# Sliding-window attention layers on one core: the first group of heads of each chunk issued within the chunk before it

## The chip, the cores and the metric

The kernel runs on one core of one Trainium2 chip. The metric is the device time of one execution in microseconds (us); lower is better. PE is the matrix engine (TensorE), DVE the vector engine, ACT the scalar engine, POOL is GpSimd, and SP only issues DMA transfers.

## The reference

Two blocks add up. The first is a gated attention over 4 sequences of 1024 tokens, 16 heads, a window of 64. The second is what the change touches: two transformer layers (`F_DEPTH = 2`), width 256, 8 heads of 64, a window of 128 keys back. Each layer computes

```
h = shift_token(x);  q, k, v = h @ wqkv          # 256 -> 3 x 512
q, k = l2norm(q) * qs, l2norm(k) * ks; rotary positions (xpos) on both
o = softmax(mask(q @ k.T)) @ v                   # per head, local windows
x = x + o @ wo                                   # 512 -> 256
h = layernorm(shift_token(x))
a, g = split(h @ w1 + b1)                        # 256 -> 2 x 682
x = x + (a * gelu(g)) @ w2 + b2                  # 682 -> 256
```

All data is float32. The projections split each operand into a high and a low part and add three products.

## The kernel before

**Two phases.** `attention_phase` does the gated block; the change leaves it alone. `layers_phase` does the two layers for 4 sequences each, so 8 iterations (`it`, `SEQUENCES`), and every iteration has two chunks (`HALVES`) of 512 tokens: 16 chunks in all. A chunk is four tiles of 128 tokens.

**One written order.** The list `ORDER` names the steps of a chunk. Each engine walks through the whole list and does only its own part of each step, in that order; semaphores do the rest. So an engine that waits at one step holds up all its later steps. A step `(kind, a)` counts over both chunks of an iteration.

**The chunk's work.** Attention goes over 8 groups (`UNITS`): 4 pairs of heads times 2 pairs of tiles. For group `a`: `scores` is the product of queries and keys on PE (L1494) and the masked maximum on DVE (L1737); `softmax` is the exponential on ACT (L1649); `weigh` is the reciprocal of the row sums on DVE (L1745) and the scaling on POOL (L1370); `transpose` brings the probabilities across on PE (L1505, L1509) with copies on ACT (L1590, L1593, L1594); `values` multiplies with the values on PE (L1527). `project_o` is the output projection. Then the feed-forward part: `ln_stats`, `ln_apply`, `transpose_h`, 12 steps `up` (L1552) and 12 steps `down` (L1567), and `out` (DVE, L1809), which adds the result to the residual.

**Work for the chunk after.** Within a chunk, the queries, keys and values of the following one are made: `transpose_x` (PE L1422, high part ACT L1602, low part DVE L1688), `project_qk` (PE L1415, ACT L1614 and L1620, DVE L1693), `rope` and `rope_sum`, `transpose_qk` (PE L1466, copied out by ACT L1596 in two copies, queries and keys), `project_v`.

**Buffers that tie the engines.** The scores of even groups lie in one pair of PSUM banks and those of odd groups in another; that second pair is `y_banks` as well, in which `down` adds up. Three more banks (`bank`, handed out in turn by `take_bank`) take the results of all the other PE steps; a fill waits until the fill three before it has been read out. `project_qk`, `transpose`, `transpose_x` and `transpose_qk` take two fills, `project_v` and `up` one.

**The chunk's end.** The order ends with ..., `up 10`, `up 11`, `down 7` to `down 9`, `transpose_qk 3`, `down 10`, `down 11`, `out 0`, `out 1`, and the following chunk starts with `scores 0`, `scores 1`, `transpose_x 0`, `scores 2`, `transpose 0`, `transpose 1`. On DVE `out 1` waits for `down 11`. On PE `scores 0` waits for all four `transpose_qk`, `scores 1` for `out 1`, and `scores 2` for the exponential of group 0.

Of the kernel before, what the change touches and what calls it, by code (L numbers as in the profile page):

```python
# [214 lines left out]
def attention_phase(nc, kept, x, gamma, w_qkv, w_gates, b_gates, w_out, masks, identity, states, attended,  # L215
                    layer_weights, split_weights, tables_in, tables_out, q_scale, k_scale, rows_in, rows_out):

    with ExitStack() as ctx:
# [626 lines left out]
        def _(dve):  # L845
# [127 lines left out]
F_PREPARE = ("load_wqkv", "load_tables", "transpose_x", "project_qk", "rope", "rope_sum", "transpose_qk", "project_v", "cross_values")  # L973
F_FIRST_HALF = ("shift_keys", "load_wqkv", "load_others")
ORDER = [("softmax", 0), ("scores", 0), ("scores", 1), ("weigh", 0), ("weigh", 1), ("softmax", 1), ("load_x1", 0), ("transpose_x", 0),
         ("scores", 2), ("transpose", 0), ("softmax", 2), ("transpose", 1), ("load_x", 0), ("scores", 3), ("weigh", 2), ("project_qk", 0),
         ("weigh", 3), ("softmax", 3), ("rope", 0), ("scores", 4), ("values", 0), ("values", 1), ("take_o", 0), ("transpose", 2),
         ("project_qk", 1), ("scores", 5), ("weigh", 4), ("rope_sum", 0), ("softmax", 4), ("transpose", 3), ("project_qk", 2),
         ("values", 2), ("scores", 6), ("weigh", 5), ("load_tables", 0), ("load_others", 0), ("shift_keys", 0), ("rope", 1), ("softmax", 5),
         ("values", 3), ("transpose_qk", 0), ("take_o", 1), ("transpose", 4), ("softmax", 6), ("scores", 7), ("shift_front", 0),  # L980
         ("weigh", 6), ("project_qk", 3), ("project_o", 0), ("transpose", 5), ("softmax", 7), ("rope_sum", 1), ("weigh", 7), ("values", 4),
         ("values", 5), ("take_o", 2), ("transpose", 6), ("project_v", 0), ("transpose_qk", 1), ("transpose", 7), ("ln_stats", 0),
         ("ln_apply", 0), ("take_o", 3), ("rope", 2), ("values", 6), ("values", 7), ("project_v", 2), ("transpose_h", 0), ("project_o", 1),
         ("rope_sum", 2), ("up", 0), ("up", 1), ("ln_stats", 1), ("up", 2), ("project_v", 1), ("down", 0), ("down", 1), ("project_v", 3),
# [6 lines left out]
def layers_phase(nc, kept, attended_end, states, attended, out, wqkv_in, wo_in, w1_in, w2_in, rows_in, tables_in, masks):  # L991
# [3 lines left out]
    with ExitStack() as ctx:  # L995
# [333 lines left out]
        def _(pool):  # L1329
# [565 lines left out]
```

## Time and profile before

| | |
|---|---|
| median of 3 runs | 1958.6 us (1950.5 to 1962.69) |
| the profiled execution: own time | 1963.61 us |
| its span, first to last instruction | 1961.8 us |
| granted TensorE clock, mean | 0.981 of full speed |
| the layers' part of the span | about 707 to 1961 us |
| PE busy | 94% of the span |
| ACT, DVE, POOL busy | 70%, 64%, 47% |

The profile is one execution. Busy shares are over the whole span; they do not tell which engine holds up a given stretch, so the views that follow are cut to the end of one chunk. A row of the timeline reads: start in us, duration, engine, line of the kernel, operation, what it writes and reads, how many, and in brackets how long the engine was idle before it and what ended that. A PE row that joins many matmuls ends about 0.2 us after the next one could start, since matmuls overlap.

### The profile page before, as it was taken

How to read it: one execution, taken by the hardware profiler on the slowest of the kernel's cores; microseconds unless marked ns; L12 is line 12 of the kernel's file. 1: busy time of each engine (PE TensorE's matmuls, PEld its weight loads, DVE VectorE, ACT ScalarE, POOL GpSimd, SP SyncE). 2: the span in 40 equal slices, each digit the busy share in tenths (PEclk: the TensorE clock that was granted, in tenths of full speed). 3: DMA queues.
4: the chain of work that ended last, by engine and by line, in shares of the span. 5: the costliest groups of instructions: out<-in, count | busy, mean ns of one | idle time of the engine just before them, and what ended most of it. 6: DMA issues, size and time to landing. Idle time of an engine off the chain costs nothing.

```text
span 1961.8 us, 47822 instructions
## 1 busy us (share of the span) xinstructions
PE 1842.9 (94%) x17808; PEld 1567.0 (80%) x17808; DVE 1246.3 (64%) x4125; ACT 1376.9 (70%) x3997; POOL 922.5 (47%) x1315
## 2 busy tenths in 40 slices
PE   6999999999999689999999999999999999999998
PEld 4788788788788469788788897887888878878777
DVE  4544543454443367777777777677777777777765
ACT  5886987878688365866757758667576585775764
POOL 2533543444344454636536446355364563654632
PEclk9999999999999889999999999999999999999999
DMA  4321320322324610110110101304112112010110
GB/s 146 99 76 56 116 87 34 116 76 77 88 78 146 196 41 23 47 55 23 47 43 24 55 15 53 122 15 166 39 39 63 34 47 65 25 54 25 44 45 28
DMA packets 127003, 128.91 MB, mean 66 GB/s; under 512 B 28112, under 2 KB 101940, under 8 KB 126772
## 3 DMA queue, kind: packets, MB, share of 16 engines
q1 hardware_dynamic: 123604, 119.56, 19.7%
q10 hardware_dynamic: 3168, 6.29, 0.9%
q8 instruction: 142, 2.33, 0.5%
q14 instruction: 89, 0.73, 0.1%
HBM read 72.84 MB, written 37.25 MB: 56 GB/s over the span
## 4 chain that ended last, share of the span: by engine, by line
PE 41%; DVE 11%; ACT 11%; issue 1%; POOL 1%; DMA 1%; SPq 0%; DVEq 0%; ACTq 0%; POOLq 0%
PE f_bank L1415 17%; PE f_bank L1552 7%; PE f_o_bank L1527 4%; PE f_scores L1567 4%; PE f_scores L1494 3%; ACT f_prob L1649 3%; DVE f_u L1803 3%; DVE f_gu L1799 2%; PE f_bank L1505 2%; ACT f_u L1669 2%; PE f_bank L1466 2%; PE f_bank L1509 1%; ACT f_probT L1590 1%; DVE f_actT L1688 1%; ACT f_probT L1594 1%
## 5 line engine op out<-in xcount | busy, mean ns | idle before, releaser
L594 POOL TENSOR_SCALAR a_prob<-a_prob,a_row_inv,a_gate 128x128 f32<-128x128 f32 x512 | 227.6, 468 | 377.7 <-DVE a_row_inv L932 377.7
L1370 POOL TENSOR_SCALAR f_prob<-f_prob,f_row_inv 128x192 f32<-128x192 f32 x512 | 214.5, 443 | 291.6 <-DVE f_row_inv L1745 291.6
L1415 PE MATMUL f_bank<-weights,f_actT 128*128 128x512 f32 x1152 | 302.9, 409 | 5.4 <-DVE f_norm L1693 3.9
L1552 PE MATMUL f_bank<-f_hT,f_w 128*128 128x256 f32 x2112 | 270.2, 283 | 5.4 <-DVE f_gu L1799 5.4
L1552 PEld LDWEIGHTS f_bank<-f_hT,f_w 128*128 128x128 f32 x2112 | 259.4, 189 | 10.3 <-DVE f_gu L1799 8.9
L1415 PEld LDWEIGHTS f_bank<-weights,f_actT 128*128 128x128 f32 x1152 | 211.7, 193 | 55.4 <-DVE f_norm L1693 7.7
L1352 POOL TENSOR_TENSOR f_qk_tok<-f_qk_tok,tables 128x512 f32<-128x512 f32 x128 | 165.1, 1313 | 158.4 <-DVE f_sin_part L1705 158.4
L1649 ACT ACTIVATE f_prob<-f_scores,f_neg_max 128x192 f32<-128x192 f32 x512 | 208.5, 428 | 14.1 <-DVE f_neg_max L1737 12.8
L1346 POOL TENSOR_TENSOR f_norm<-f_norm,f_minus_half 128x16 f32<-128x16 f32 x64 | 199.3, 3115 | 34.0 <-DVE f_norm L1697 32.4
L1669 ACT ACTIVATE f_u<-f_gu 128x256 fp32r<-128x256 f32 x192 | 80.3, 418 | 191.2 <-DVE f_gu L1799 191.2
L824 ACT ACTIVATE a_prob<-a_scores,a_neg_max 128x128 f32<-128x128 f32 x512 | 179.9, 392 | 24.0 <-DVE a_neg_max L923 17.0
L615 PE MATMUL a_bank<-a_xT,weights 128*128 128x512 f32 x768 | 195.0, 404 | 1.5 <-DVE a_wgate L901 1.5
L1737 DVE CUSTOM_DVE_ANT_0 f_scores<-f_scores,f_mask 128x192 f32<-128x192 f32 x512 | 166.2, 387 | 36.4 <-PE f_scores L1494 36.1
L1803 DVE TENSOR_TENSOR f_u<-f_gu,f_u 128x256 fp32r<-128x256 f32 x192 | 114.5, 596 | 93.0 <-ACT f_u L1669 93.0
L615 PEld LDWEIGHTS a_bank<-a_xT,weights 128*128 128x128 f32 x768 | 142.5, 190 | 36.7 <-issue 2.9
L1567 PE MATMUL f_scores<-f_w,f_u 128*128 128x256 f32 (+1 forms) x1088 | 153.3, 285 | 0.6 <-DVE f_u L1803 0.3
L923 DVE CUSTOM_DVE_ANT_0 a_scores<-a_scores,a_mask 128x128 f32<-128x128 f32 x512 | 129.9, 325 | 25.8 <-PE a_scores L689 25.8
L1567 PEld LDWEIGHTS f_scores<-f_w,f_u 128*128 128x128 f32 (+1 forms) x1088 | 139.5, 189 | 5.3 <-DVE f_u L1803 3.8
L1494 PEld LDWEIGHTS f_scores<-f_kT,f_q 64*64 64x64 f32 x3072 | 101.1, 140 | 43.6 <-ACT f_prob L1649 19.8
L1494 PE MATMUL f_scores<-f_kT,f_q 64*64 64x128 f32 (+2 forms) x3072 | 120.0, 290 | 16.2 <-ACT f_prob L1649 15.5
L1665 ACT ACTIVATE f_gu<-f_bank,f_rows 128x256 f32<-128x256 f32 x192 | 89.8, 468 | 53.3 <-PE f_bank L1552 52.0
L1693 DVE TENSOR_REDUCE f_norm<-f_square 128x8 f32<-128x512 f32 x128 | 86.0, 683 | 61.4 <-ACT f_square L1620 61.3
(139 smaller groups left out, 3988.8 us busy)
## 6 DMA issues: line engine op xcount, KB each, us to landing
split_weights<-a_hi_lo SPq DMA_DIRECT2D x16, 512.0 KB
x_next<-states SPq DMA_DIRECT2D x32, 256.0 KB, 4.4
tables<-scaled_tables SPq DMA_DIRECT2D x16, 512.0 KB, 5.4
f_x<-states SPq DMA_DIRECT2D x16, 512.0 KB, 3.8
split_weights<-a_hi_lo SPq DMA_DIRECT2D x12, 682.0 KB
weights<-split_weights ACTq DMA_DIRECT2D x6, 1024.0 KB, 9.9
f_w<-split_weights SPq DMA_DIRECT2D x4, 1280.0 KB, 10.6
f_v_crossed<-f_v SPq DMA_DIRECT2D x40, 128.0 KB, 2.3
```

What stands on the lines that cost most here:

```text
L594: last = nc.gpsimd.tensor_scalar(part, part, row_inv[:, a % 2, head, t:t + 1], gate[:, half, t, h:h + 1], ALU.mult, ALU.mult)
L615: last = nc.tensor.matmul(out, lhs(c, a), rhs(c, b), start=(i == 0), stop=(i == len(order) - 1))
L824: e = nc.scalar.activation(prob[:, a % 2, head, t, :], scores[a % 2][head][:, t, :], ACT.Exp, bias=neg_max[:, a % 2, head, t:t + 1], scale ...
L1346: nc.gpsimd.tensor_tensor(n, n, minus_half[:], ALU.pow).then_inc(norm_ready.sem, 1)
L1370: last = nc.gpsimd.tensor_scalar(part, part, row_inv[:, a % 2, head, t:t + 1], 1.0, ALU.mult, ALU.mult)
L1415: last = nc.tensor.matmul(out, lhs(c, a), rhs(c, b), start=(i == 0), stop=(i == len(order) - 1))
L1494: mm = nc.tensor.matmul(scores[a % 2][head][queries, t, place:place + keys.stop - keys.start], q[rows, pair, col:col + P][:, queries], kT[ ...
L1552: mm = nc.tensor.matmul(out[:, which * PART:(which + 1) * PART], w1[:, wp, c, col:col + P], hT[:, hp, c, columns_of(a // FH)], start=(i == ...
L1567: mm = nc.tensor.matmul(y_banks[a // FH % PARTS][:, t, :], u[0:k, a % GATED, up, t * P:(t + 1) * P], w2[0:k, wp, j, :], start=(j == 0 and ...
L1649: last = nc.scalar.activation(prob[:, a % 2, head, t, :], scores[a % 2][head][:, t, 0:KEYS], ACT.Exp, bias=neg_max[:, a % 2, head, t:t + 1 ...
L1737: last = nc.vector.tensor_tensor_reduce(out=sc, in0=sc, in1=mask[:, t + 1 if half or tile or t else 0], scale=-1.0, scalar=3e38, op0=ALU.a ...
L1803: nc.vector.tensor_tensor(place, gu[0:m, a % 2, :], u[0:m, a % GATED, HI, :].bitcast(F32), ALU.subtract).then_inc(u_ready.sem, 1)
```

## The change

**What is moved.** Group 0 of the following chunk becomes step 8 of the chunk: `scores 8`, `softmax 8` and `weigh 8` stand at the end of `ORDER`, and `scores 0`, `softmax 0`, `weigh 0` are gone from its start. `transpose_qk 3`, which stood between `down 9` and `down 10`, now stands after `down 11`. The other steps of the list are placed anew as well; per engine the order is, apart from group 0 and `transpose_qk 3`:

```
PE:   values 2 goes from behind project_qk 2 to ahead of transpose 3; the rest as before
ACT:  ... up 11, softmax 8, transpose_qk 3 | softmax 1, transpose_x 0, transpose 0 ...
      (before: ... up 11, transpose_qk 3 | softmax 0, softmax 1, transpose_x 0, transpose 0 ...)
DVE:  ... up 11, out 0, out 1, scores 8, weigh 8 | scores 1, weigh 1, transpose_x 0 ...
      (before: ... up 11, out 0, out 1 | scores 0, scores 1, weigh 0, weigh 1, transpose_x 0 ...)
POOL: weigh 8 comes last in the chunk, weigh 1 first in the following one
SP:   load_x1, load_tables, load_others, shift_front, shift_back, load_x, cross_values, shift_keys,
      add_attended, out  (before: load_x second, shift_keys ahead of shift_front)
```

**The waits.** The first group waits only for the first two tiles of queries and keys, group 4 for all four. Waits for weights and rows that are loaded once in a layer are made once in a layer.

```diff
+F_ATTENTION = ("scores", "softmax", "weigh")
...
-         ("transpose_qk", 3), ("down", 10), ("down", 11), ("out", 0), ("out", 1), ("load_wqkv", 0)]
+ORDER = [("scores", 1), ("weigh", 1), ("softmax", 1), ("transpose_x", 0), ("scores", 2), ("transpose", 0), ("softmax", 2), ("transpose", 1),
...
+         ("up", 6), ("up", 7), ("down", 4), ("up", 8), ("up", 9), ("rope_sum", 3), ("down", 5), ("down", 6), ("x1_bias", 0),
+         ("add_attended", 0), ("transpose_qk", 2), ("up", 10), ("up", 11), ("out", 0), ("out", 1), ("scores", 8), ("load_wqkv", 0),
+         ("softmax", 8), ("down", 7), ("down", 8), ("down", 9), ("down", 10), ("down", 11), ("weigh", 8), ("transpose_qk", 3)]
...
-                  ("transpose_qk", t0 + 3)]
+                  ("transpose_qk", t0 + 3), ("scores", NU), ("softmax", NU), ("weigh", NU)]
...
             half, s = divmod(a, UNITS)
-            return half, s % PAIRS, s // PAIRS * 2
+            return half % HALVES, s % PAIRS, s // PAIRS * 2
...
+        def before_unit(it, a):
+
+            sequence, unit = started(it, a - 2)
+            return sequence, ("scores", unit)
+
+        def started(it, a):
+
+            return (it, a) if a else (it - 1 if it else None, NU)
...
+        LAYER_STARTS = (0, BATCH)
...
                 elif kind == "project_qk":
                     if a % TILES == 0:
-                        pe.wait_ge(kept.weights_loaded[QUERY], loads(1, layer))
-                        pe.sem_inc(pe_carried, 1)
+                        if fresh:
+                            pe.wait_ge(kept.weights_loaded[QUERY], loads(1, layer))
+                            pe.sem_inc(pe_carried, 1)
                         pe.wait_ge(emptied.sem, emptied.past(it, ("transpose_x", a // TILES), CT - 1))
                     for which in (QUERY, KEY):
-                        if which == KEY and a % TILES == 0:
+                        if which == KEY and a % TILES == 0 and fresh:
                             pe.wait_ge(kept.weights_loaded[KEY], loads(1, layer))
                             pe.sem_inc(pe_carried, 1)
...
                 elif kind == "project_v":
-                    pe.wait_ge(kept.weights_loaded[2], loads(1, layer))
+                    if fresh:
+                        pe.wait_ge(kept.weights_loaded[2], loads(1, layer))
...
+            def take_scores(it, a):
+
+                half, pair, tile = unit_place(a)
+                chunk, s = divmod(a, UNITS)
+                if s == 0:
+
+                    pe.wait_ge(copied.sem, copied.past(it, ("transpose_qk", (chunk - 1) * TILES + 1), 1))
+                    if half:
+                        pe.wait_ge(keys_shifted.sem, keys_shifted.past(it, ("shift_keys", 0)))
+                elif s == 1:
+                    pe.wait_ge(x2_ready.sem, x2_ready.upto(it, 2 * half - 1))
+                elif s == PAIRS:
+
+                    prepared_in = it if half else it - 1 if it else None
+                    pe.wait_ge(copied.sem, copied.past(prepared_in, ("transpose_qk", (half or HALVES) * TILES - 1), 1))
+
+                if s == 1 and a < UNITS:
+                    pe.wait_ge(exped.sem, exped.past(it - 1, ("scores", NU - 1), 1) if it else exped.upto(None, -1))
+                elif it is not None:
+                    pe.wait_ge(exped.sem, exped.past(*before_unit(it, a), 1))
+                for t in (0, 1):
...
+                mm.then_inc(scored.sem, 1)
```

`weigh` (POOL), `softmax` (ACT), `masked_max` and `invert` (DVE) are the bodies of before, moved into functions so that the list `before` can call them too. `before`, the steps ahead of the first iteration, gets the first group of the first chunk; the last iteration leaves out its `scores 16`.

## Rows read from the trace of the kernel before

**Rows 1.** The page, part 1: busy time, share of the span and instructions of each engine.

```profile
...
PE 1842.9 (94%) x17808; PEld 1567.0 (80%) x17808; DVE 1246.3 (64%) x4125; ACT 1376.9 (70%) x3997; POOL 922.5 (47%) x1315
...
```

**Rows 2.** What PE waited for between 780 and 1962 us: total us, times, longest.

```profile
...
PE f_scores L1494 <- ACT f_prob L1649: 15.5, 17, 2.0
PE f_bank L1505 <- POOL f_prob L1370: 12.6, 32, 1.2
...
PE f_bank L1509 <- DVE f_actT L1688: 4.2, 14, 0.3
PE f_bank L1415 <- DVE f_norm L1693: 3.7, 14, 0.3
...
```

**Rows 3.** All engines in order of time at one chunk's end, 1416.3 to 1424.5 us.

```profile
...
1416.41 0.60 ACT L1596 ACTIVATE f_q<-f_bank 128x512 f32<-128x512 f32 x1
...
1416.87 1.49 DVE L1809 TENSOR_TENSOR f_x<-f_scores,f_x 128x512 f32<-128x512 f32 x2
...
1416.90 0.59 ACT L1596 ACTIVATE f_kT<-f_bank 128x512 f32<-128x512 f32 x1
1417.51 1.28 ACT L1649 ACT_TABLE_LOAD   x1
...
1417.56 1.75 PE L1494 MATMUL f_scores<-f_kT,f_q 64*64 64x192 f32 x48
...
1418.71 0.37 DVE L1737 CUSTOM_DVE_ANT_0 f_scores<-f_scores,f_mask 128x192 f32<-128x192 f32 x1 [0.36 <-PE f_scores L1494]
...
1419.23 1.09 PE L1422 MATMUL f_bank<-ident,x_next 128*128 128x128 f32 x8
...
1419.48 0.42 ACT L1649 ACTIVATE f_prob<-f_scores,f_neg_max 128x192 f32<-128x192 f32 x1 [0.69 <-DVE f_neg_max L1737]
...
1421.24 0.18 DVE L1745 RECIPROCAL f_row_inv<-f_row_sum 128x4 f32<-128x4 f32 x1
...
1421.26 0.89 PE L1494 MATMUL f_scores<-f_kT,f_q 64*64 64x192 f32 x24 [0.93 <-ACT f_prob L1649]
...
1421.62 3.24 POOL L1370 TENSOR_SCALAR f_prob<-f_prob,f_row_inv 128x192 f32<-128x192 f32 x8 [12.92 <-DVE f_row_inv L1745]
...
1422.27 0.45 ACT L1649 ACTIVATE f_prob<-f_scores,f_neg_max 128x192 f32<-128x192 f32 x1
...
1422.59 0.41 PE L1505 MATMUL f_bank<-ident,f_prob 128*128 128x128 f32 x2 [0.45 <-POOL f_prob L1370]
1422.67 1.12 ACT L1602 ACTIVATE f_actT<-f_bank 128x512 fp32r<-128x512 f32 x2
...
1422.85 0.18 DVE L1745 RECIPROCAL f_row_inv<-f_row_sum 128x4 f32<-128x4 f32 x1 [1.44 <-ACT f_prob L1649]
...
1423.34 1.29 DVE L1688 TENSOR_TENSOR f_actT<-f_bank,f_actT 128x512 fp32r<-128x512 f32 x2 [0.31 <-ACT f_actT L1602]
...
1424.09 0.44 PE L1509 MATMUL f_bank<-ident,f_prob 128*128 128x128 f32 x2 [0.34 <-DVE f_actT L1688]
...
```

**Rows 4.** PE at the third tile's query product of the same chunk.

```profile
...
1437.63 3.06 PE L1415 MATMUL f_bank<-weights,f_actT 128*128 128x512 f32 x12 [0.27 <-DVE f_norm L1693]
...
```

**Rows 5.** Four chunks, `out` to `out`: length, busy us (instructions), clock, DMA, GB/s.

```profile
...
1495.87:1574.13 78.26, 74.49 (x736) 64.65 (x736) 59.13 (x165) 54.07 (x151) 42.18 (x48) 1.00 0.16 48
1653.16:1732.89 79.73, 76.01 (x737) 65.71 (x736) 59.41 (x164) 54.07 (x151) 42.19 (x48) 0.98 0.16 48
1574.13:1653.16 79.03, 75.19 (x769) 65.56 (x768) 60.13 (x164) 54.39 (x151) 42.89 (x48) 1.00 0.14 43
1732.89:1813.13 80.24, 76.55 (x768) 66.69 (x768) 60.08 (x165) 54.42 (x151) 42.86 (x48) 0.98 0.14 42
...
```

**Rows 6.** Four us behind two chunk ends: length, PE busy, clock, DMA, GB/s.

```profile
...
1739.89:1743.89 4.00, 3.78 (x33) 0.57 0.99 304
1820.13:1824.13 4.00, 3.63 (x39) 1.00 0.64 241
...
```

**Rows 7.** The page, part 6: one DMA issue, KB each, us to landing.

```profile
...
x_next<-states SPq DMA_DIRECT2D x32, 256.0 KB, 4.4
...
```

More of the change, by code:

```diff
@@ L973 @@
 F_PREPARE = ("load_wqkv", "load_tables", "transpose_x", "project_qk", "rope", "rope_sum", "transpose_qk", "project_v", "cross_values")
+F_ATTENTION = ("scores", "softmax", "weigh")
 F_FIRST_HALF = ("shift_keys", "load_wqkv", "load_others")
[L975 to L984, printed above, removed]
-         ("ln_apply", 1), ("up", 3), ("down", 2), ("transpose_h", 1), ("rope", 3), ("up", 4), ("down", 3), ("up", 5), ("up", 6), ("up", 7),
-         ("down", 4), ("up", 8), ("up", 9), ("x1_bias", 0), ("rope_sum", 3), ("down", 5), ("down", 6), ("transpose_qk", 2),
-         ("shift_back", 0), ("up", 10), ("up", 11), ("down", 7), ("down", 8), ("cross_values", 0), ("down", 9), ("add_attended", 0),
-         ("transpose_qk", 3), ("down", 10), ("down", 11), ("out", 0), ("out", 1), ("load_wqkv", 0)]
@@ L1054, in layers_phase @@
                     steps.append((kind, h * PER_CHUNK[kind] + i))
-        last = [(kind, a) for kind, a in steps if kind != "load_x" and not (kind in F_PREPARE and (a >= (HALVES - 1) * PER_CHUNK[kind] or kind == "load_wqkv"))]
+        last = [(kind, a) for kind, a in steps if kind != "load_x" and not (kind in F_ATTENTION and a == NU) and not (kind in F_PREPARE and (a >= (HALVES - 1) * PER_CHUNK[kind] or kind == "load_wqkv"))]
         e, t0 = HALVES - 1, (HALVES - 1) * TILES
@@ L1360, in _ @@
                     rope(None, a)
+                elif kind == "weigh":
+                    weigh(None, a)
             def iteration(it, steps, layer):
@@ L1475, in iteration @@
                 for kind, a in steps:
[L1476 removed]
+                    ahead = a // PER_CHUNK[kind] == HALVES - 1
+                    if kind not in F_ATTENTION:
+                        prepare(it, kind, a, next_layer if ahead else layer, ahead and it == BATCH - 1)
                     if kind == "scores":
[L1478 to L1497 removed]
+                        take_scores(it, a)
                     elif kind == "transpose":
@@ L1628, in _ @@
                     take_raw(None, a)
+                elif kind == "softmax":
+                    softmax(None, a)
             def iteration(it, steps, layer, next_layer):
@@ L1726, in _ @@
                     rope_sum(None, a)
-            dve.wait_ge(consts_loaded, 16 * CONSTS)
+                elif kind == "scores":
+                    dve.wait_ge(consts_loaded, 16 * CONSTS)
+                    masked_max(None, a)
+                elif kind == "weigh":
+                    invert(None, a)
             def iteration(it, steps, layer):
```

123 lines of the change are left out of this document (68 added, 55 removed).

## The prediction

> **What bounds the kernel now.** I began with the page: PE is busy 94% of the span, no other engine over 70% [rows 1]. So what a change in the order can win is PE's idle time, and what it can lose is more of it. The second view is what PE waited for in the layers [rows 2]. The reader should see that the waits are few and all alike: 15.5 us in 17 waits of `scores` for ACT's exponential, 12.6 us in 32 waits of `transpose` for POOL, 4.2 us in 14 waits of L1509 for the low part of `transpose_x` on DVE, and 3.7 us in 14 waits of a query product for DVE's sums of squares. 14, 32 and 17 against 15 chunk ends say where they lie: the first three repeat at every chunk end, the fourth once in a chunk.
>
> The third view is one such end in order of time [rows 3]. PE runs through `scores 0` and `scores 1` (from 1417.56), then `transpose_x` (from 1419.23), is idle 0.93 us until `scores 2` at 1421.26, idle 0.45 before the first transpose at 1422.59, and waits again for L1509 at 1424.09. What ends that last wait is a chain on other engines: masked maximum on DVE at 1418.71, eight exponentials on ACT from 1419.48 to 1422.67 (groups 0 and 1, 0.40 each), `transpose_x` high part on ACT at 1422.67, its low part on DVE at 1423.34, then L1509. PE's own work in that stretch is cover, not the limit. Idle per end: 0.93 + 2 x 12.6/32 + 4.2/14 = 2.0 us.
>
> **The change part by part.**
>
> *The masked maximum of group 0.* It now follows `out 1` directly. DVE ends `out 0` and `out 1` at 1416.87 + 1.49 = 1418.36 and then waits 0.36 us for `scores` on PE [rows 3]. With the scores done before `down 7`, that wait goes and nothing more: `out 1` stands ahead of `scores 8` in DVE's order and waits for `down 11`. So on DVE, and behind it on ACT and POOL, group 0 does not lie inside the preceding chunk. Gain 0.35 us per end. What is late next is `out 1` itself.
>
> *PE around it.* `scores 8` takes the place of `transpose_qk 3` between `up 11` and `down 11`. Two groups of scores take 1419.23 - 1417.56 = 1.67 us, 0.84 each; eight transposes show as 1.09 with 0.2 of tail, so about 0.87 [rows 3]. The swap moves `down 11` by 0.03 us at most; I cost it at nothing. The downs that lose this cover still have `scores 8` in its place.
>
> *The copies of `transpose_qk 3`.* Here I see the cost. On ACT they stand at 1416.41 and 1416.90, while ACT has nothing else to do: the exponential waits 0.69 us for DVE even after them [rows 3]. After the change they stand behind `softmax 8`, which waits for the masked maximum, and ahead of `softmax 1`. They enter the chain. Queued behind them on ACT are `softmax 1`, `transpose_x` and the copies of `transpose 0`; and PE's second fill of `transpose_x` waits for the first copy, since it gets that bank.
>
> By the rows: the maximum starts at 1418.36, the exponential 0.77 later as now (1419.48 - 1418.71) at 1419.13, its four parts end at 1420.73, and the copies, 0.49 each (from 1416.41 to 1416.90), at 1421.71.
>
> *The reciprocal ahead of the second maximum.* DVE now does `weigh 8` before `scores 1`. The fourth part of the exponential starts at 1420.33; the reciprocal follows such a start by 0.58 (1422.27 to 1422.85), so 1420.91; it takes 0.18; the maximum of group 1 follows, and its exponential 0.77 later: 1421.86. That is a shade later than the copies allow. The exponential of group 1 therefore starts at 1421.86, against 1419.48 + 4 x 0.40 = 1421.08 now: 0.78 later. Everything behind it moves as one: high part, low part, L1509. POOL starts `weigh 8` earlier, but `weigh 1`, which the second transpose needs, starts with that same 0.78.
>
> Bounds: if the reciprocal overlaps the next maximum by half, 0.69; if both copies cost the 0.61 that the second shows before the table load, 1421.95 and so 0.87. I take 0.78, by the rows of the same instructions. Over 15 ends: 11.7 us. At the last of them `transpose_x` is absent, but POOL's `weigh 1` sets the same shift. For the start of the first chunk, which no row here shows, I allow -1 to +1 and take 0.
>
> *The table load.* ACT loads the exponential's table in 1.28 us at 1417.51, and the exponential starts 1.97 us after that start, held by DVE [rows 3]. After the change the load stands directly behind `up 11`, at 1416.41, and costs nothing. The Trainium skill, "ScalarE: Activation LUTs", section "What ACT_TABLE_LOAD costs", counts a drain on top, 2.66 us for a switch. By that the load would be what binds now (1417.51 + 2.66 = 1420.17), moving it up would win 1.04 instead of 0.35 per end, and the sum would be about 10 us better. The row has an exponential at 1419.48, so it disagrees, and I go by the row.
>
> *`values 2` ahead of `transpose 3`.* PE waits 0.27 us at 1437.63 for a bank that DVE empties [rows 4]; the moved step takes longer than that and fills the gap. Gain: all of the 3.7 us [rows 2]. Bound: 0 if its own operand were late.
>
> *Waits made once in a layer.* They are for data that landed long before; no row of [rows 2] names such a wait. Cost and gain 0; bound of gain 2 us.
>
> *SP's order.* `load_x` and its two transfers, 4.4 us to landing [rows 7], go behind `shift_back`, and `cross_values` and `shift_keys` behind them. `transpose_x` needs the rows only in the following chunk; the DMA engines are busy 0.14 to 0.16 of a chunk [rows 5], and that is the cover. If it were gone, `ln_stats 1` would wait up to those 4.4 us. I take 0.
>
> *The clock.* The granted clock behind a chunk end is 0.57 to 0.73 at eleven of the ends and 1.00 at four, all in the second layer; one of each kind is in [rows 6]. The levels are 1.2 and 2.4 GHz. What it costs: chunks alike but for that take 79.73 against 78.26 and 80.24 against 79.03, so 1.2 to 1.5 us [rows 5]. In front of every fall stand the idle pieces above. The change lengthens them, from 2.0 to 2.8 us per end, with one piece of about 1.6 before the second half of `transpose_x`. Bounds: none of the four further ends falls (0), all do (5.4), or low stretches get twice as long (15 x 1.35 = 20 more). I take two of four: 2.7.
>
> **Sum.** 11.7 - 3.7 + 2.7 = +10.7 us. Against the profiled execution's own 1963.6 (its span of 1961.8 with 1.8 around it) that is 1974.3. The median of the runs is 5.0 below that execution, so 1958.6 + 10.7 = 1969.
>
> **The rivals.**
>
> *A, the forecast:* copies in the chain, clock a little worse. 1962 to 1977. Chance 0.53.
>
> *B, the clock decides.* The longer idle pieces let the clock fall behind all ends, and for longer at most of them: 8.0 + 5.4 + 10 to 20, so 1982 to 1992; in its mildest form 1979. For it: eleven of fifteen fall already. Against it: four ends with the very same idle pieces did not fall. Chance 0.25.
>
> *C, faster: the copies stay off the path.* If the bank and ACT's queue are no limit after all, because `scores 2` and POOL's first scaling, both 0.35 us earlier, are what set the pace, the end becomes 15 x 0.35 = 5.3 shorter; with the 3.7 that is -9.0, 1950. It decides where the delay at L1509 is under 3.7/15 = 0.25 us. For it: PE waits for ACT and POOL are three quarters of the idle time [rows 2]. Against it: L1509 waits too, last in the chain. Chance 0.17.
>
> *D, the change does what it is called.* Attention of the following chunk really runs beside the feed-forward part and all idle pieces at the ends go: 15 x 2.0 + 3.7 = 34 us, 1925. It needs the masked maximum ahead of `out 1`, which DVE's order excludes. Chance 0.05. The Trainium skill, "Perfetto Trace Analysis", section "Optimization Strategy", says that interleaving regimes with different limits may improve performance; that speaks for D, and the order of [rows 3] does not let it happen here.
>
> **The numbers.** About 1% is what a measurement of this kernel tells from no change: 1939 to 1978. D is faster (0.05), A and C are within (0.70), B is slower (0.25). The range takes in A, C and the lower part of B: 1949 to 1984. A alone is 1962 to 1977.
>
> **What would show it.** In the timeline of a chunk end after the change: the masked maximum directly behind `out 1`, without a wait; the two copies of L1596 between the fourth and fifth exponential; a PE gap of about 1.6 us within `transpose_x` and `scores 2` about 0.5 us later after `out 0` than now (4.39 us); L1509 8.0 us after the start of `out 0` instead of 7.22. The wait of 0.27 at the third query product gone. Chunks 0.5 us longer at equal clock; 1.00 behind fewer than four ends. I am wrong if the copies are found before the exponential, if L1509 comes earlier than 7.22, or if a chunk's length changes by something that does not sit at its end.

## The result

The changed kernel takes 1962.9 us, the median of 19 executions (1960.8 to 1965.8); the kernel before took 1957.8 on the same chip (19 executions, 1950.5 to 1962.7). The ratio is 1.0033, with a 95% interval of 1.0025 to 1.0041: 5 us slower, within 1%. The prediction was 1969 with a range of 1949 to 1984. Case A stood at 1962 to 1977, so the time is at its lower edge. That it lies there is partly luck: the order of the work cost more than forecast, the granted clock gave time back where it was forecast to cost some, and the two errors nearly cancel.

Waits of PE in the layers of the changed kernel (us in total, times, longest), to be held against [rows 2]:

```profile
PE f_bank L1445 <- ACT f_q L1637: 19.4, 14, 1.4
PE f_bank L1550 <- DVE f_actT L1735: 18.8, 14, 1.3
PE f_bank L1546 <- POOL f_prob L1379: 10.9, 19, 1.3
...
PE f_scores L1519 <- ACT f_prob L1668: 1.5, 1, 1.5
...
```

The exponential's 15.5 us are gone but for the 1.5 at the last end, and so are the 3.7 for the sums of squares. In their place stand two waits of a new kind, for the copies of `transpose_qk 3` (1.4 each end) and for the low part of `transpose_x` (1.3).

One chunk end in order of time (start, duration, engine, line), where [rows 3] showed the end before. `out` is now L1868, the masked maximum L1773, the exponential L1668, the copies L1637, the reciprocal L1781, and the transpose that closed the chain, L1509, is L1550:

```profile
1411.13 1.28 ACT L1668 ACT_TABLE_LOAD   x1
1411.14 0.42 DVE L1862 TENSOR_TENSOR f_u<-f_gu,f_u 42x256 fp32r<-42x256 f32 x1 [0.48 <-ACT f_u L1716]
1411.59 1.49 DVE L1868 TENSOR_TENSOR f_x<-f_scores,f_x 128x512 f32<-128x512 f32 x2
...
1413.00 0.35 DVE L1773 CUSTOM_DVE_ANT_0 f_scores<-f_scores,f_mask 128x192 f32<-128x192 f32 x1
...
1415.36 0.61 ACT L1637 ACTIVATE f_q<-f_bank 128x512 f32<-128x512 f32 x1
1415.51 0.18 DVE L1781 RECIPROCAL f_row_inv<-f_row_sum 128x4 f32<-128x4 f32 x1 [1.15 <-ACT f_prob L1668]
1415.67 0.37 DVE L1773 CUSTOM_DVE_ANT_0 f_scores<-f_scores,f_mask 128x192 f32<-128x192 f32 x1
1415.83 0.62 ACT L1637 ACTIVATE f_kT<-f_bank 128x512 f32<-128x512 f32 x1
...
1416.02 0.66 PE L1445 MATMUL f_bank<-ident,x_next 128*128 128x128 f32 x4 [1.38 <-ACT f_q L1637]
...
1416.44 0.42 ACT L1668 ACTIVATE f_prob<-f_scores,f_neg_max 128x192 f32<-128x192 f32 x1
...
1419.43 0.44 PE L1550 MATMUL f_bank<-ident,f_prob 128*128 128x128 f32 x2 [1.34 <-DVE f_actT L1735]
```

The order is the predicted one: maximum directly behind `out 1`, copies between the fourth exponential and the fifth (1416.44), a PE gap of 1.38 (forecast: about 1.6) inside `transpose_x`. The idle pieces of PE at an end sum to 2.7 us instead of 2.0. L1550 starts 7.84 us behind `out 0`; before it was 7.22.

Two chunks of the second layer, `out` to `out` (length, busy us and instructions of PE, PEld, DVE, ACT, POOL, then clock, DMA share, GB/s), against [rows 5]:

```profile
1411.59:1492.23 80.64, 75.25 (x770) 65.59 (x768) 60.41 (x164) 54.20 (x151) 43.92 (x48) 1.00 0.14 42
1492.23:1570.76 78.53, 74.15 (x738) 64.65 (x736) 59.28 (x165) 53.88 (x151) 42.04 (x48) 1.00 0.16 48
```

The two chunks of an iteration differ in length: one has about 770 PE instructions, the other about 738. At a clock of 1.00 the short kind is 0.27 us longer than before (78.53 against 78.26), near the 0.35 that the chunk end gives: +0.62, less the 0.27 of the query product. The long kind is 1.6 longer (80.64 against 79.03). That is not at its end, but 41 us behind it:

```profile
1446.25 2.64 POOL L1379 TENSOR_SCALAR f_prob<-f_prob,f_row_inv 128x192 f32<-128x192 f32 x4
...
1447.39 1.22 DVE L1759 TENSOR_TENSOR f_qk_tok<-f_qk_tok,f_sin_part 128x1024 f32<-128x1024 f32 x1
...
1448.71 1.25 DVE L1762 TENSOR_TENSOR f_qk_tok<-f_qk_tok,f_norm 128x1024 f32<-128x1024 f32 x1
1448.87 3.87 POOL L1362 TENSOR_TENSOR f_norm<-f_norm,f_minus_half 128x16 f32<-128x16 f32 x1
...
1452.73 1.79 POOL L1379 TENSOR_SCALAR f_prob<-f_prob,f_row_inv 128x192 f32<-128x192 f32 x4
1453.69 0.41 PE L1546 MATMUL f_bank<-ident,f_prob 128*128 128x128 f32 x2 [0.71 <-POOL f_prob L1379]
...
1454.58 0.44 PE L1546 MATMUL f_bank<-ident,f_prob 128*128 128x128 f32 x2 [0.47 <-POOL f_prob L1379]
```

PE waits 0.71 + 0.47 us in the seventh transpose for POOL's `weigh 7`, because `weigh 6` took 2.64. The same place before the change shows 1.66 and no wait:

```profile
1450.90 1.66 POOL L1370 TENSOR_SCALAR f_prob<-f_prob,f_row_inv 128x192 f32<-128x192 f32 x4
...
1452.48 1.22 DVE L1712 TENSOR_TENSOR f_qk_tok<-f_qk_tok,f_sin_part 128x1024 f32<-128x1024 f32 x1
1452.49 3.98 POOL L1346 TENSOR_TENSOR f_norm<-f_norm,f_minus_half 128x16 f32<-128x16 f32 x1
```

Last, the clock behind two chunk ends of the changed kernel, the second being the one end where it falls ([rows 6] are those of before):

```profile
1417.59:1421.59 4.00, 2.50 (x36) 1.81 (x35) 2.74 (x11) 3.68 (x14) 1.62 (x4) 1.00 0.57 211
1894.83:1898.83 4.00, 2.67 (x16) 1.70 (x20) 1.53 (x9) 3.96 (x17) 1.62 (x4) 0.56 0.22 76
```

The granted clock stays at 1.00, the upper level of 2.4 GHz, behind 14 of the 15 ends; before the change it fell behind eleven. So at equal clock seven chunks cost 1.5 more and seven 0.3 more, 12.6 us; the last, shorter one 1.6 more (68.08 against 66.45, its clock lower in both). The two spans differ by -0.9, which leaves about 15 us to have come back; 10 falls fewer at the 1.2 to 1.5 each of [rows 5] would be 12 to 15. The profiled execution before was slower than any of the 19 (1963.6 against at most 1962.7), which is why the medians show +5 where the two profiled executions show -0.9. More falls than usual would explain it, but the clocks of those 19 are not on record.

### The profile page after: what moved, and what is told of

The parts are those of the page before. It is cut to its first block, busy times and chain, and to the rows that moved or that the text cites. A ratio compares the mean times of both kernels' runs of the same rounds, so it can differ in the third digit from the quotient of the medians.

```text
span 1960.9 us, 47748 instructions
## 1 busy us (share of the span) xinstructions
PE 1828.5 (93%) x17808; PEld 1558.8 (79%) x17808; DVE 1250.1 (64%) x4125; ACT 1372.4 (70%) x3997; POOL 928.6 (47%) x1315
## 4 chain that ended last, share of the span: by engine, by line
PE 35%; DVE 12%; ACT 11%; POOL 5%; issue 4%; DVEq 0%; SPq 0%; POOLq 0%; ACTq 0%
PE f_bank L1438 14%; PE f_bank L1593 7%; PE f_scores L1608 4%; ACT f_prob L1668 4%; PE f_o_bank L1568 3%; DVE f_u L1862 3%; PE f_scores L1519 3%; DVE f_gu L1858 2%; POOL f_prob L1379 2%; PE f_bank L1546 2%; ACT f_u L1716 2%; POOL f_norm L1362 1%; POOL f_qk_tok L1368 1%; DVE f_actT L1735 1%; DVE f_scores L1773 1%
## 5 line engine op out<-in xcount | busy, mean ns | idle before, releaser
L1379 POOL TENSOR_SCALAR f_prob<-f_prob,f_row_inv 128x192 f32<-128x192 f32 x512 | 220.0, 449 | 288.6 <-DVE f_row_inv L1781 288.6
L1593 PEld LDWEIGHTS f_bank<-f_hT,f_w 128*128 128x128 f32 x2112 | 259.6, 189 | 10.9 <-DVE f_gu L1858 9.5
L1668 ACT ACTIVATE f_prob<-f_scores,f_neg_max 128x192 f32<-128x192 f32 x512 | 208.3, 424 | 25.0 <-DVE f_neg_max L1773 23.8
L1773 DVE CUSTOM_DVE_ANT_0 f_scores<-f_scores,f_mask 128x192 f32<-128x192 f32 x512 | 166.9, 387 | 20.8 <-PE f_scores L1519 20.7
L1608 PE MATMUL f_scores<-f_w,f_u 128*128 128x256 f32 (+1 forms) x1088 | 149.0, 285 | 0.3 <-DVE f_u L1862 0.3
L936 DVE TENSOR_TENSOR a_o<-a_o_bank,a_o 128x512 fp32r<-128x512 f32 x64 | 44.1, 689 | 118.7 <-ACT a_o L831 118.7
```

Source lines behind the costliest of these rows:

```text
L1379: last = nc.gpsimd.tensor_scalar(part, part, row_inv[:, a % 2, head, t:t + 1], 1.0, ALU.mult, ALU.mult)
L1593: mm = nc.tensor.matmul(out[:, which * PART:(which + 1) * PART], w1[:, wp, c, col:col + P], hT[:, hp, c, columns_of(a // FH)], start=(i == ...
L1608: mm = nc.tensor.matmul(y_banks[a // FH % PARTS][:, t, :], u[0:k, a % GATED, up, t * P:(t + 1) * P], w2[0:k, wp, j, :], start=(j == 0 and ...
L1668: last = nc.scalar.activation(prob[:, a % 2, head, t, :], scores[a % 2][head][:, t, 0:KEYS], ACT.Exp, bias=neg_max[:, a % 2, head, t:t + 1 ...
L1773: last = nc.vector.tensor_tensor_reduce(out=sc, in0=sc, in1=mask[:, t + 1 if half or tile or t else 0], scale=-1.0, scalar=3e38, op0=ALU.a ...
```

## The experiments

Twelve kernels ran, in groups of four on a chip each; the kernel before took 1958.8, 1957.9 and 1961.6 in the three groups. So the ratios compare best; a difference of two medians from different groups can hold some 4 us of the chip. "Norms late" means that POOL does the norms of `project_qk 3` behind `weigh 7` (e2). The chunk lengths are those of the second layer.

| run | median us | ratio to before, 95% | mean clock | long, short chunk at 1.00 |
|---|---|---|---|---|
| before | 1957.8 to 1961.6 | 1 | 0.982 | 79.03, 78.26 |
| after | 1962.9 | 1.0033 (1.0025 to 1.0041) | 0.989 | 80.5, 78.5 |
| e1 `values 2` alone | 1961.2 | 1.0012 (1.0000 to 1.0025) | 0.984 | 79.92, 78.02 |
| e11 the same, norms late | 1956.3 | 0.9993 (0.9978 to 1.0007) | 0.982 | 78.58, 78.01 |
| e2 after, norms late | 1954.4 | 0.9976 (0.9963 to 0.9989) | 0.989 | 79.17, 78.48 |
| e3 copies back | 1999.3 | 1.0199 (1.0183 to 1.0215) | 0.973 | none |
| e5 reciprocal back | 1958.5 | 1.0005 (0.9992 to 1.0018) | 0.990 | 80.44, 78.51 |
| e4 both back | 1959.6 | 1.0003 (0.9989 to 1.0018) | 0.987 | 80.12, 78.21 |
| e6 maximum before `out` | 1968.3 | 1.0051 (1.0030 to 1.0072) | 0.984 | 80.05, 78.13 |
| e8 early maximum, norms late | 1962.0 | 1.0021 (1.0007 to 1.0035) | 0.985 | 79.33, 78.61 |
| e16 before, transposes twice | 1956.5 | 0.9974 (0.9963 to 0.9986) | 0.986 | 79.02, 78.37 |
| e14 e11, transposes twice | 1950.8 | 0.9941 (0.9927 to 0.9954) | 0.987 | 78.64, 78.00 |
| e13 e5, norms late | 1951.8 | 0.9945 (0.9932 to 0.9957) | 0.989 | 79.13, 78.45 |
| e10 e4, norms late | 1949.5 | 0.9933 (0.9920 to 0.9946) | 0.988 | 78.86, 78.18 |

The mean clock is over all executions of a run; within the kernel before, 0.001 of it goes with 1.05 to 1.75 us, by the group; 1.35, used below, is a middle value and what rests on it an estimate.

### Where the long chunks come from

**e1_values2_alone.** The kernel before, with this in its order:

```diff
-("softmax", 4), ("transpose", 3), ("project_qk", 2), ("values", 2), ("scores", 6)
+("softmax", 4), ("values", 2), ("transpose", 3), ("project_qk", 2), ("scores", 6)
```

> The kernel before with one part of the change: in the order, `values 2` stands ahead of `transpose 3` and `rope_sum 0`. My step (0.27 us per chunk): the wait of 0.27 us of the query product for DVE's sums of squares goes, 3.7 us over the layers, and each chunk is 0.27 shorter at equal clock. Rival (the move costs elsewhere): the step gives POOL or DVE another place in the chunk, and the seventh transpose then waits for POOL's `weigh 7` in every other chunk, as in the changed kernel; then at least 7 of the chunks are about 1 us longer than now and the sum is +3 to +4.

The rival was right, by the chunks; the time itself hardly shows it (the interval of the ratio begins at 1.0000). The wait of 0.27 is gone and the short chunks are 0.24 shorter, but the long ones are 0.9 longer. POOL is not late here:

```profile
1446.84 2.66 POOL L1370 TENSOR_SCALAR f_prob<-f_prob,f_row_inv 128x192 f32<-128x192 f32 x4
...
1447.99 1.22 DVE L1712 TENSOR_TENSOR f_qk_tok<-f_qk_tok,f_sin_part 128x1024 f32<-128x1024 f32 x1
...
1449.47 3.87 POOL L1346 TENSOR_TENSOR f_norm<-f_norm,f_minus_half 128x16 f32<-128x16 f32 x1
```

`weigh 6` starts 34.03 us behind `out 0` (1412.81), exactly as before (1450.90 - 1416.87). DVE's addition comes 0.43 earlier: 1.15 us behind `weigh 6` instead of 1.58. `weigh 6` is four scalings of about 0.41, so the fourth starts 1.2 us in. With 1.58 it is under way before the addition; with 1.15 the addition is first, the fourth scaling stands until it ends (1447.99 + 1.22 = 1449.21) and finishes at 1449.5. In the changed kernel the distance is 1.14, so there too it is the `values 2` move that makes the long chunks, not the chunk end. The short chunks are spared because their distance there is 1.38, and the fourth scaling starts first:

```profile
1525.96 1.63 POOL L1379 TENSOR_SCALAR f_prob<-f_prob,f_row_inv 128x192 f32<-128x192 f32 x4
...
1527.34 1.32 DVE L1759 TENSOR_TENSOR f_qk_tok<-f_qk_tok,f_sin_part 128x1024 f32<-128x1024 f32 x1
```

The Trainium skill, "SBUF — State Buffer", section "SBUF: two separate sides", has the rule: a DVE instruction with two SBUF inputs and a GpSimd instruction that reads SBUF take a shared port as a lock, and whichever comes second stands for the whole of the first. For POOL behind DVE the rows agree, with 1.0 us per meeting. For DVE behind POOL they show less than the whole: the addition above takes 1.32 instead of 1.22, and the DVE instruction that starts inside the norms before the change (L1715 at 1453.81, the norms from 1452.49 to 1456.47) takes its usual 1.23. Before the change the norms met the addition and paid it (3.98); now `weigh 6` pays it once and the norms once more, on L1762 (3.87).

**e2_norms3_behind_weigh7.** The changed kernel; POOL skips the norms of tile 3 at their place and does them behind `weigh 7`:

```diff
 if kind == "weigh":
     weigh(it, a)
+    if a % UNITS == UNITS - 1 and ("project_qk", late) in steps:
+        norms(it, late)
 elif kind == "project_qk":
-    norms(it, a)
+    if a % TILES != TILES - 1:
+        norms(it, a)
```

> The changed kernel with one thing moved: POOL computes the norms of `project_qk 3` (3.87 us) behind its `weigh 7` instead of ahead of it. Theory (POOL's chain of `weigh 4` to `weigh 7` ends 0.62 us later behind the chunk end, and in every other chunk its `weigh 6` then runs beside DVE's addition of `rope_sum 1` and takes 2.64 instead of 1.66 us): the waits of 0.71 and 0.47 us of transpose 7 for `weigh 7` go, seven chunks become 1.1 us shorter, sum -7 to -8 against the changed kernel, 1955. Rival 1 (the time only shifts): the norms are now late for `rope 3` or for `transpose_qk`, and the wait shows there; 0. Rival 2 (the extra 1.1 us is not POOL's): the waits go and the chunks stay as long as they are; 0.

Faster by 8.6 us in the medians and by 11 in the ratios (0.9976 against 1.0033), against 7 to 8 in the theory; seven chunks of 1.33 are 9.3:

```profile
1442.62 2.63 POOL L1379 TENSOR_SCALAR f_prob<-f_prob,f_row_inv 128x192 f32<-128x192 f32 x4
...
1447.23 1.63 POOL L1379 TENSOR_SCALAR f_prob<-f_prob,f_row_inv 128x192 f32<-128x192 f32 x4 [1.98 <-DVE f_row_inv L1785]
1448.82 2.92 POOL L1362 TENSOR_TENSOR f_norm<-f_norm,f_minus_half 128x16 f32<-128x16 f32 x1
```

`weigh 6` still takes 2.63, but POOL is now idle for 1.98 before `weigh 7`, which comes in time. The norms meet no addition and take 2.92, the price without a collision. The expectation's reason, POOL late by 0.62, is wrong: in e1 POOL is not late and the chunks are long all the same. The cure did not depend on it.

**e11_values2_norms3.** The edits of e1 and e2 together, on the kernel before.

> The kernel before with `values 2` ahead of `transpose 3` and POOL's norms of `project_qk 3` behind its `weigh 7`. Alone, the first made seven chunks 0.9 us longer (79.9 against 79.0 at equal clock), with POOL's `weigh 6` at 2.66 instead of 1.66 us beside DVE's addition of `rope_sum 1`, and the others 0.22 shorter. Theory (that overlap and what it delays is the whole of it): `weigh 6` still takes 2.6, but `weigh 7` no longer stands behind the norms; no wait for it is left, both kinds of chunk are 0.22 to 0.27 shorter than in the kernel before, so about -5.5 against the run with `values 2` alone, 1955 to 1956. Rival (the longer chunks come from PE's own order, the scaling is only seen beside it): seven chunks stay near 79.9, 1961.

Both kinds of chunk are now shorter than before, by 0.45 and 0.25 (78.01), and POOL is busy for 42.73 us of the long one instead of the 43.78 of e1 (before: 42.86):

```profile
1409.33:1487.91 78.58, 75.09 (x768) 65.57 (x768) 60.10 (x165) 54.19 (x151) 42.73 (x48) 1.00 0.14 43
```

The median gains 4.9 on e1 (theory: 5.5), the ratio 0.19%, or 3.7 us. Seven chunks of 1.34 are 9.4, and the clock, 0.982 against 0.984, takes a part of it. Why the long kind gains 0.18 beyond the 0.27 is not traced.

### What sets the chunk end

**e3_transpose_qk3_back** and **e4_both_back**, from the changed kernel:

```diff
-("softmax", 8), ("down", 7), ("down", 8), ("down", 9), ("down", 10), ("down", 11), ("weigh", 8), ("transpose_qk", 3)]
+("down", 7), ("down", 8), ("down", 9), ("transpose_qk", 3), ("softmax", 8), ("down", 10), ("down", 11), ("weigh", 8)]
```

and in e4 also `weigh 8` gone from there, with `("weigh", 0)` behind `("scores", 1)`.

> The changed kernel with `transpose_qk 3` back between `down 9` and `down 10`, and ACT's exponential of group 0 behind its copies, so that the copies stand ahead of the chain and not in it; the reciprocal stays ahead of the second maximum. Theory of the prediction (both paths, copies and reciprocal, end at nearly the same time, so that taking away one gives little): PE's idle piece of 1.38 us inside `transpose_x` goes, L1550 comes no more than 0.1 us earlier behind the start of `out 0` than the 7.84 of the changed kernel; sum 0 to -2. Rival (the copies alone are the delay): L1550 comes 0.4 to 0.6 earlier, 15 x 0.5 = -7.5.

> The changed kernel with both taken out of the chain: `transpose_qk 3` as before the change, and the reciprocal and POOL's scaling of group 0 behind the maximum of group 1. Theory (0.62 us of delay per end is copies and reciprocal together, and the masked maximum directly behind `out 1` is a gain of its own of 0.35 to 0.43): L1550 at 6.8 us behind the start of `out 0` against 7.84 now and 7.22 before the change; POOL is no longer late, so that the waits of transpose 7 for `weigh 7` go too; 15 x 1.05 + 7 x 1.1 = -23 against the changed kernel at equal clock, 1940; if the granted clock falls again behind eleven of the ends as before the change, 11 x 1.35 = +15, so 1955. Rival (something else sets the end, as `scores 2` or POOL's first scaling): L1550 at 7.2 or later, -9 at equal clock, 1954 to 1969.

Neither kernel takes only the copies off the chain: with `scores 8` still ahead of `down 7`, the transposes now delay `down 11`. One end of e3:

```profile
1434.12 0.69 DVE L1868 TENSOR_TENSOR f_x<-f_scores,f_x 128x512 f32<-128x512 f32 x1
...
1435.66 0.69 DVE L1868 TENSOR_TENSOR f_x<-f_scores,f_x 128x512 f32<-128x512 f32 x1 [0.84 <-PE f_scores L1608]
...
1436.27 0.36 DVE L1773 CUSTOM_DVE_ANT_0 f_scores<-f_scores,f_mask 128x192 f32<-128x192 f32 x1
...
1439.72 0.42 ACT L1668 ACTIVATE f_prob<-f_scores,f_neg_max 128x192 f32<-128x192 f32 x1 [0.97 <-DVE f_neg_max L1773]
...
1442.70 0.69 PE L1550 MATMUL f_bank<-ident,f_prob 128*128 128x128 f32 x2 [1.42 <-DVE f_actT L1735]
```

`out 1` waits 0.84 (0.11 in the changed kernel), and PE 0.78 for the bank that it empties, so everything behind `out 1` is 0.73 late. Counted from `out 0`, L1550 comes at 8.58, less that 0.73 at 7.85, against 7.84: the copies alone are worth nothing. In e4, with the reciprocal out as well, the end is this (`out 0` at 1408.56; L1772 is the maximum, L1667 the fifth exponential, L1549 the transpose):

```profile
1410.71 0.35 DVE L1772 CUSTOM_DVE_ANT_0 f_scores<-f_scores,f_mask 128x192 f32<-128x192 f32 x1
...
1413.07 0.43 ACT L1667 ACTIVATE f_prob<-f_scores,f_neg_max 128x192 f32<-128x192 f32 x1
...
1416.06 0.44 PE L1549 MATMUL f_bank<-ident,f_prob 128*128 128x128 f32 x2 [0.34 <-DVE f_actT L1734]
```

The transpose comes at 7.50, less 0.73 at 6.77: together the two are worth 1.07 (theory 1.05). Counted from the masked maximum, nothing has to be taken off: the fifth exponential follows it by 2.38 before the change, 3.44 in the changed kernel, 3.45 in e3 and 2.36 in e4. So the prediction's reading of two paths that end together holds. By the chunks, e4 is 0.3 to 0.4 shorter than the changed kernel, 1.07 less the 0.73; its 7.50 and its 1959.6 are the rival's figures, but the late outputs make them, not `scores 2` or POOL. The clock is, by estimate, the greater part of e3's time: it falls behind every end, here to 0.50, the lower level of 1.2 GHz:

```profile
1444.12:1448.12 4.00, 4.00 (x32) 3.16 (x31) 1.80 (x13) 2.90 (x12) 0.00 (x0) 0.50 0.00 0
```

The mean clocks, 0.973 against 0.989, stand for some 22 of the 36 us at 1.35 per 0.001; the later L1550, 8.58 against 7.84 at each of 14 ends, for 10; about 4 are left over. The waits for `weigh 7` stayed in e4, with the addition 1.14 behind `weigh 6`: the step that e1 explains.

**e5_reciprocal_back.** Only the reciprocal and `weigh 8` moved back.

> The changed kernel with one thing taken back: the reciprocal and POOL's scaling of group 0 stand behind the maximum of group 1 again; the copies of `transpose_qk 3` stay between the two exponentials. Theory (copies and reciprocal end together, each alone sets the 0.62 us of an end): L1549 stays at 7.7 to 7.84 us behind the start of `out 0`, sum 0 to -2 against the changed kernel, 1961 to 1963. Rival (the reciprocal alone is the delay, the copies fit beside the maximum): L1549 at 7.4 or less, 15 x 0.45 = -7. The waits of 0.71 and 0.47 us for `weigh 7` stay in every other chunk in both.

```profile
1416.32 0.45 ACT L1667 ACTIVATE f_prob<-f_scores,f_neg_max 128x192 f32<-128x192 f32 x1
...
1419.33 0.44 PE L1549 MATMUL f_bank<-ident,f_prob 128*128 128x128 f32 x2 [1.25 <-DVE f_actT L1734]
```

L1549 is 7.75 behind `out 0` (1411.58): the second copy ends and the exponential begins 0.1 earlier, as the theory has it. The median, 1958.5, is 2.5 below it; the profiled execution was the slowest of the twelve (1962.2), with the chunks of the changed kernel, so I can't say where that lies. By the ratios it is more: 1.0005 (0.9992 to 1.0018) against 1.0033 (1.0025 to 1.0041), some 5 us, and e13 against e2 below shows as much again, 0.9945 against 0.9976. The 0.1 at 14 ends is 1.3 us; what gives the rest is open.

**e6_maximum_before_out.** The condition of case D:

```diff
-("out", 0), ("out", 1), ("scores", 8), ("load_wqkv", 0)
+("scores", 8), ("out", 0), ("out", 1), ("load_wqkv", 0)
```

> The changed kernel with `scores 8` ahead of `out 0` and `out 1` in the order, so that DVE's masked maximum of group 0 stands ahead of both outputs: the condition that case D of the prediction named. Case D: group 0 then lies inside the preceding chunk and the idle pieces of the ends go, 15 x 2 = -30, 1933. Theory (what was ahead of the first maximum comes behind it: the outputs now stand between the maximum of group 0 and PE's `scores 1`, which wants the bank that `out 1` empties): the exponential of group 0 starts about 1.4 us earlier behind the DVE's subtraction for `up 11`, `scores 1` and the maximum of group 1 come 1.3 later, so the copies are off the chain but L1550 is no earlier than now by more than 0.3; -5 to +8, 1958 to 1971.

```profile
1415.85 1.28 ACT L1668 ACT_TABLE_LOAD   x1
1416.20 0.35 DVE L1773 CUSTOM_DVE_ANT_0 f_scores<-f_scores,f_mask 128x192 f32<-128x192 f32 x1
...
1417.14 0.42 ACT L1668 ACTIVATE f_prob<-f_scores,f_neg_max 128x192 f32<-128x192 f32 x1
...
1423.74 0.44 PE L1550 MATMUL f_bank<-ident,f_prob 128*128 128x128 f32 x2 [1.59 <-DVE f_actT L1735]
```

Case D falls. Group 0 does run inside the preceding chunk, but the outputs now stand between it and `scores 1`. Counted from DVE's subtraction for `up 11` (1415.86), L1550 comes at 7.88 against 8.29, 0.4 earlier, and the chunks are 0.4 shorter. The clock falls again (0.984), and the median is 5.4 longer. The clock's 0.005 would be some 7 us by the estimate; in the profiled execution another 4.0 lie ahead of the layers' first `out 0` (787.95 against 783.97), and no run shows why.

### The clock

**e16_transposes_twice.** The kernel before:

```diff
-for t in range(TILES):
+twice = list(range(TILES)) if kind == "transpose_x" and it is not None and c == CT - 1 else []
+for t in twice + list(range(TILES)):
     last = nc.tensor.transpose(out[:, t * P:(t + 1) * P], source[:, t, c * P:(c + 1) * P], ident[:])
```

> The kernel before, with work added that computes nothing new: PE does the four transposes of the second half of `transpose_x` twice into the same bank, 0.55 us of PE work in the idle piece of 0.93 us ahead of `scores 2` at every chunk end but the last. By waits alone nothing changes. Theory (these idle pieces are what the granted clock falls behind): with the piece cut to about 0.4 us the falls become fewer than the eleven of the profiled execution before, each worth 1.2 to 1.5 us; if all go, the chunks are 79.0 and 78.2 everywhere and the time is 1947 to 1951. Rival 1 (the falls have nothing to do with this piece): as before the change, 1957 to 1959. Rival 2 (the extra transposes delay `scores 2`, or the high part in ACT): +2 to +4, 1960 to 1962.

The repeated transposes write the same values again. 5.1 us faster (0.9974), with the long chunks at 1.00 unchanged (79.02), the short ones 0.1 to 0.4 longer, and the idle piece ahead of `scores 2` at 0.50 instead of 0.93:

```profile
1416.78 0.89 PE L1495 MATMUL f_scores<-f_kT,f_q 64*64 64x192 f32 x24 [0.50 <-ACT f_prob L1650]
```

PE does more work and the kernel is shorter. The mean clock rises from 0.982 to 0.986. So filling this piece makes the granted clock fall less, here and again in e14. The falls become fewer, not none: in the profiled execution five of the layers' first 14 chunks are still under 1.00, against ten before, and the time stays short of the theory's 1947 to 1951. The piece is not all that decides: e1 and e11 have the same pieces as the kernel before, and in their profiled executions the clock falls behind four and five of the 14 ends.

**e14_values2_norms3_twice.** The same on e11.

> The run with `values 2` ahead of `transpose 3` and POOL's norms behind `weigh 7` (chunks of 78.57 and 78.01 at clock 1.00, but 0.96 or 0.98 in five of the layers' first eight, 1956.3), with the same doubled transposes as in the other kernel of this group. Theory (clock and order add up): if the falls go, both kinds of chunk stay at their length at clock 1.00 and the fast executions of that kernel, 1949.4, become the rule: 1947 to 1950, the best so far. Rival (falls stay): 1956.

1950.8, at the edge of the theory: clock 0.987 instead of 0.982, and a ratio of 0.9941 instead of 0.9993.

### Candidates

**e8_early_maximum_norms.** Both back, norms late, and `scores 8` between `up 7` and `down 4`; `shift_keys`, which it needs, is placed earlier.

> A candidate built from the changed kernel: `scores 8` stands between `up 7` and `down 4`, so that the masked maximum of group 0 is done before `up 11` is; the copies of `transpose_qk 3` and the reciprocal stand where they stood before the change; POOL's norms of `project_qk 3` behind `weigh 7`. Theory (what sets the end is then DVE's outputs, PE's `scores 1` behind `out 1`, and ACT's table load of 1.28 us ahead of the first exponential): the first exponential starts at the end of the table load, 1.9 to 2.0 us behind the start of `out 0`, L1549 at 6.3 to 6.6, against 7.84 in the changed kernel: 15 x 1.3 + 7 x 1.3 = -28, 1935 if the granted clock stays at 1.00 behind the ends, 1945 to 1950 if it falls behind most of them. Rival (`scores 1` waits for `out 1` and sets the maximum of group 1, whatever group 0 does): L1549 at 7.2 to 7.5, 1945 to 1955.

```profile
1409.31 1.50 DVE L1872 TENSOR_TENSOR f_x<-f_scores,f_x 128x512 f32<-128x512 f32 x2
...
1409.96 1.28 ACT L1671 ACT_TABLE_LOAD   x1
...
1411.25 0.42 ACT L1671 ACTIVATE f_prob<-f_scores,f_neg_max 128x192 f32<-128x192 f32 x1
...
1415.84 0.44 PE L1553 MATMUL f_bank<-ident,f_prob 128*128 128x128 f32 x2
```

L1553 comes at 6.53, as the theory has it, and the time, 1962.0, is that of neither. The chunks are 79.33 and 78.61, no shorter than e2's. `scores 8` was 0.84 us of PE work behind `up 11`, under which ACT and DVE prepared `down 11`; moved ahead, it shortens the path behind `out 0` and lengthens the one in front. That is argued from the lengths (1.3 less behind `out 0`, the chunk 0.16 longer than e2's) and was not taken apart. `out 0` is no fixed point to count from once PE's work moves across it, which the expectation overlooks.

**e13_recip_norms** and **e10_both_back_norms**: e5 and e4 with the norms behind `weigh 7`.

> A candidate from the changed kernel: the reciprocal of group 0 back behind the maximum of group 1 (alone 1958.5) and POOL's norms of `project_qk 3` behind `weigh 7` (alone 1954.35). If the two add: 1962.9 - 4.4 - 8.5 = 1950. If the reciprocal's place gives nothing of its own (its chunks had the length of the changed kernel's, 80.5 and 78.5): 1954. In both the clock stays at 1.00 behind all ends but the last, and seven chunks are 79.1 to 79.2 instead of 80.5.

> The kernel with both the copies and the reciprocal taken out of the chain (1959.6; chunks 80.2 and 78.2 at clock 1.00), with POOL's norms of `project_qk 3` behind `weigh 7` as well. Theory (its seven long chunks are long by the same overlap of POOL's scaling with DVE's addition): the waits for `weigh 7` go, these chunks are 79.0, 7 x 1.2 = -8.4, 1951. Rival (POOL is not late in it, and the 80.2 has another source): 1959. Either way the clock falls behind some ends, as it did there.

e13 lies between its two expectations, with e2's chunks. e10 beats both kernels: 0.9933 of the kernel before, 1.3 us off the long chunks of e4. Its lead on e13 does not lie in the chunks: from the layers' first `out 0` to their last both take 1163 us, but e10 reaches the first at 779.57 and e13 at 784.04. e10, e14 and e13 can't be told apart by their intervals.

## Why the prediction was right in its time, and where it was wrong

*The masked maximum.* Right: it follows `out 1` without a wait, at 1.41 behind the start of `out 0` instead of 1.84, a gain of 0.43 where I had 0.35.

*The copies and the reciprocal.* The mechanism is as told and the size was too large: 0.62 at L1550, not 0.78. The extra 0.08 of the maximum is half of that; the reciprocal overlaps its neighbours by more than I allowed, so the second maximum starts at 1415.67, 0.16 behind it. Over the 14 ends that have an L1550 that is 8.7 us instead of 10.9 (11.7 with the fifteenth). The bounds, 0.69 to 0.87, were too narrow. That either alone holds the end where it is, is shown by e3 (0.0) and e5 (0.1), and that the two together make the delay by e4 (1.07).

*`values 2` ahead of `transpose 3`.* This step failed. It won its 0.27 and moved DVE's addition 0.43 towards POOL's `weigh 6`, which e1 shows to cost 0.9 in every long chunk, with its own gain already taken off. I had costed the moved step by what waits for it on PE, and not by what the engines behind PE then do side by side. "A chunk's length changes by something that does not sit at its end" was my own sign of being wrong, and it came.

*The clock.* This step failed as well, in its sign: +2.7 forecast, and about -9 in the medians (0.989 against 0.982 or 0.983, at 1.35 us per 0.001). Case B, to which I gave 0.25, rested on the same idea, that longer idle pieces make it fall more often. The pieces did become longer (1.38 and 1.34) and it fell at one end instead of eleven. The prediction names against case B that four ends with the same idle pieces did not fall; its own term of +2.7 leaves that out of account: the sum of the pieces alone doesn't decide. The -9 is an estimate from the mean clocks, no run isolates it. One figure of case B follows from none of its terms: without longer falls they give 8.0 + 5.4, so 1972, and not the 1979 of its mildest form.

*The table load.* Nothing, as costed, since DVE ends the wait. In e6 and e8 the maximum is early, and the load itself binds: the exponential starts 1.29 us behind its start in both. The Trainium skill, "ScalarE: Activation LUTs", section "What ACT_TABLE_LOAD costs", would have 2.66 with its drain; these rows disagree.

*Waits once per layer, SP's order.* No run took them apart. They and all else that was placed anew leave little room: against e1's chunks those of the changed kernel are 0.58 and 0.50 longer (80.50 and 78.52 against 79.92 and 78.02), where the chunk end alone gives 0.62. Nothing in the waits after points to them: none names a load, apart from what stood there before.

*Cases C and D.* C asked for under 0.25 at L1550; it is 0.62. D fell in e6, where its condition, the maximum ahead of `out 1`, is met and the kernel is slower.

So 8.7 - 3.7 + 8.3 (seven long chunks at 1.18) = +13.3 of order, which the chunk lengths give as 12.6, and -9 of clock. Together that is +4, and the medians show +5. The forecast's +10.7 had no 8.3, and the clock with the wrong sign.

## What to carry to other kernels

A step moved on PE also moves the engines that it feeds against those that it does not: before costing it, look for a POOL instruction and a DVE instruction with two SBUF operands that end up less than one instruction apart. Put the POOL work that nobody waits for soon behind the one that PE needs next. And compare chunks of equal clock before naming the cause of a difference: here order and clock were larger than the 5 us and of opposite sign.

## What the runs showed of the hardware

- One meeting of a DVE two-operand addition (1.22 us) with POOL costs POOL 1.0 us and DVE nothing when DVE is first: a scaling step goes from 1.63 to 2.64, the norms from 2.92 to 3.87 or 3.98. The addition 1.14 us behind the start of the four scalings meets the fourth, at 1.38 it does not. No row here shows DVE standing for a whole POOL instruction.
- Whether the granted clock falls behind an end is partly left to chance (1949.4 to 1960.8 for e11, with mean clocks of 0.985 to 0.979) and does not go by the idle time alone. Two long pieces of 1.38 and 1.34 (or 1.25) with 2 us of work between them, in the changed kernel, e2, e5 and e13: no fall in 14 ends of the profiled executions. Two long pieces of 0.87 and 1.59, in e6: five falls. Pieces of 0.93, 0.45, 0.30 and 0.34: ten falls before, four in e1, five in e11. Pieces of 0.78, 0.48, 0.44, 0.30 and 0.34, in e4 and e10: four and three. The same with 1.42 in place of the 0.34, in e3: a fall at every one of them. What tells them apart is open; no run was made for it.
